# ScalarE's copies of C moved to the front of their slots, and TensorE's B of the next unit moved in front of the last tile of C

## Time and profile before

| | |
|---|---|
| median of 3 runs | 381.95 us (381.24 to 383.88) |
| the profiled execution | 382.38 us, of which the span from first to last instruction is 380.6 us |
| granted TensorE clock, mean | 0.89 |
| VectorE busy | 327.5 us, 86% |
| GpSimd busy | 279.9 us, 74% |
| TensorE busy | 265.0 us, 70% |
| ScalarE busy | 230.3 us, 61% |

### The profile page before, as it was taken

How to read it: one execution, slowest core, us unless ns; L and a number is a source line. 1 busy time by engine, 2 the same in 40 slices (tenths; PEclk the granted TensorE clock), 3 DMA queues, 4 the chain that set the end, 5 groups by cost and what they waited for, 6 DMA issues and landing times.

```text
span 380.6 us, 4003 instructions
## 1 busy us (share of the span) xinstructions
PE 265.0 (70%) x1130; PEld 124.4 (33%) x1130; DVE 327.5 (86%) x365; ACT 230.3 (61%) x509; POOL 279.9 (74%) x167
## 2 busy tenths in 40 slices
PE   2557659678856788688868786878688570692791
PEld 1113123213311335133613361336223340361491
DVE  4875979999999998989999988899889999458970
ACT  3453754955596459754996488657964573154434
POOL 0092655687588998899889998998899898614642
PEclk9859898789989999789999998799969895697887
DMA  3750470190028002720092008300730000000001
GB/s 63 158 119 1 89 160 2 26 199 23 2 54 192 6 0 54 168 55 2 12 205 59 2 0 189 87 2 2 156 92 2 0 0 28 0 3 28 0 2 55
DMA packets 19246, 21.86 MB, mean 57 GB/s; under 512 B 6096, under 2 KB 15128, under 8 KB 19224
## 3 DMA queue, kind: packets, MB, share of 16 engines
q1 hardware_dynamic: 18504, 21.05, 24.4%
q10 hardware_dynamic: 720, 0.56, 0.8%
HBM read 2.72 MB, written 2.10 MB: 13 GB/s over the span
## 4 chain that ended last, share of the span: by engine, by line
PE 30%; DVE 22%; ACT 19%; issue 12%; POOL 10%; SPq 4%; DMA 3%; DVEq 0%; POOLq 0%; ACTq 0%
DVE states L1018 8%; PE ps_prep L1314 7%; DVE db L1002 5%; PE ps_b L1321 5%; ACT c_rep L559 3%; ACT ps_decay L483 3%; PE ps_y L1280 3%; SPq L440 3%; PE ps_prep L1301 3%; POOL product L756 3%; PE ps_f L1346 2%; POOL hq L812 2%; ACT r_feat L567 2%; DMA dt_rep<-dtx 2%; DVE hidden L1068 2%
## 5 line engine op out<-in xcount | busy, mean ns | idle before, releaser
L756 POOL TENSOR_TENSOR product<-states,c_rep 128x1024 f32<-128x1024 f32 x63 | 149.3, 2375 | 30.7 <-DVE states L1018 28.9
L483 ACT ACTIVATE ps_decay<-dt_rep,aneg 128x512 f32<-128x512 f32 x128 | 87.4, 692 | 43.0 <-DVE states L1018 39.9
L1002 DVE SCALAR_TENSOR_TENSOR db<-ps_b,bbc_rep,dt_rep 128x2048 f32<-128x2048 f32 x31 | 72.5, 2339 | 11.2 <-PE ps_b L1321 8.4
L1018 DVE TENSOR_TENSOR_SCAN states<-ps_decay,states,db 128x512 f32<-128x512 f32 x64 | 79.0, 1260 | 2.4 <-POOL product L756 2.4
L1018 DVE TENSOR_TENSOR_SCAN states<-ps_decay,db 128x512 f32<-128x512 f32 x64 | 75.4, 1203 | 0.4 <-ACT ps_decay L483 0.2
L1314 PE MATMUL ps_prep<-u_feat,wbc_rep 128*128 128x512 f32 x56 | 37.1, 749 | 21.0 <-ACT c_rep L559 20.9
L1321 PE MATMUL ps_b<-u_feat,wbc_rep 128*128 128x512 f32 x64 | 40.4, 719 | 15.4 <-DVE db L1002 15.4
L1280 PE MATMUL ps_y<-product,gather 128*32 128x512 f32 x256 | 36.3, 642 | 0.8 <-POOL product L756 0.8
L1346 PE MATMUL ps_f<-gate_t,xq_t 128*128 128x352 f32 x56 | 24.5, 519 | 10.2 <-DVE hidden L1068 6.1
L597 ACT ACTIVATE gate_tanh<-ps_f 128x352 f32<-128x352 f32 x28 | 13.0, 465 | 27.9 <-PE ps_f L1346 27.9
L559 ACT ACTIVATE c_rep<-ps_prep,bbc_rep 128x512 f32<-128x512 f32 x28 | 19.4, 694 | 16.7 <-PE ps_prep L1314 16.1
(11 more groups left out here) (202 smaller groups left out, 513.1 us busy)
## 6 DMA issues: line engine op xcount, KB each, us to landing
dt_rep<-dtx SPq DMA_DIRECT2D x124, 128.0 KB, 2.4
x_tok<-in_L_attn_x SPq DMA_DIRECT2D x8, 256.0 KB, 3.1
out<-y_out SPq DMA_DIRECT2D x8, 256.0 KB, 2.3
dt_rep<-dtx ACTq DMA_DIRECT2D x4, 128.0 KB, 3.7
hidden<-in_L_ffn_w_down SPq DMA_DIRECT2D x1, 176.0 KB, 3.6
x_feat<-in_L_attn_x SPq DMA_DIRECT2D x8, 0.5 KB, 2.7
hidden<-in_L_ffn_w_gate SPq DMA_DIRECT2D x1, 128.0 KB, 2.8
hidden<-in_L_ffn_w_up SPq DMA_DIRECT2D x1, 128.0 KB, 2.5
```

Source lines behind the costliest of these rows:

```text
L483: nc.scalar.activation(ps_decay[BANK_OF[k]][:], dt_rep[p][:, c, 0, :], ACT.Exp, scale=aneg[:, c, m:m + 1]).then_inc(decay_done, 1)
L756: nc.gpsimd.tensor_tensor(product[:, j % PRODUCTS], states[p][:, first:first + 2, :], over(c_rep[p][:, j // SET_PAIRS, :], 2), ALU.mult).t ...
L1002: nc.vector.scalar_tensor_tensor(out=db[m % DB][:], in0=over(ps_b[:], QUADS), scalar=bbc_rep[:, 0, m:m + 1], in1=dt_rep[p][:, :, 1, :], op ...
L1018: nc.vector.tensor_tensor_scan(out=states[p][:, k % ring, :], data0=ps_decay[BANK_OF[k]][:], data1=db[k // QUADS % DB][:, k % QUADS, :], i ...
```

## The change

ScalarE: in slots 8 to 11 (`AT["act C"]`) `prep`, the copy of a tile of C, is emitted right after the decay (and, in the first step, the first unit's C and the weights), ahead of `gate`, `square_x`, `square_h` and `down`. In all other slots `prep` stays last. TensorE: B of set 0 of the next unit moves from slot 11 to slot 10. As `spread_b` is the first call of a slot, it then stands between tile 2 of C (slot 9) and tile 3 of C (slot 10).

```diff
-    "pe x": 0, "pe conv": (1, 2), "pe z": 4, "pe B": (11, 15, 3, 7), "pe C": (7, 8, 9, 10),
+    "pe x": 0, "pe conv": (1, 2), "pe z": 4, "pe B": (10, 15, 3, 7), "pe C": (7, 8, 9, 10),
...
+                    if a is not None and k in AT["act C"]:
+                        prep(a, 1 - p, k)
                     if f is not None:
                         gate(f, k)
...
                     if h is not None:
                         down(h, 1 - p, k, ps_f2)
-                    if a is not None:
+                    if a is not None and k not in AT["act C"]:
                         prep(a, 1 - p, k)
```

## The result

The changed kernel took 391.65 us (median of 4 runs, 391.21 to 392.58) beside 382.25 us for the kernel before (4 runs, 381.24 to 383.88): a ratio of 1.0226 [1.0191, 1.0262] (in brackets, here and below, the 95% interval). The forecast was 386.3 us with 389.0 as its upper end. Six further runs of the same changed kernel had a median of 389.46 us (386.80 to 393.40), ratio 1.0131 [1.0073, 1.0189]. It is slower in both, and it spreads over 6.6 us.

The account below looks back on a forecast made before the run. No engine was full; VectorE was taken as the bound, with GpSimd's hq close behind, both releasing TensorE's slot 2 transposes. Terms 0.4 + 1.65 + 0.35 + 1.2 + 0.7 = +4.3 us gave 386.3 us, range 380.8 to 389.0.

Parts of the forecast that it names:

- The sign: Whole kernel: the change makes it slower, by +4.3 us; slower was given 0.5.
- the place: ScalarE's slot 8: the square and variance start 1.57 us late, felt at TensorE's transposes of slot 2.
- the chain: C0's wait delays square and variance, then VectorE's qh_magic and GpSimd's norm, slot 10 and hq, then TensorE's slot 2 transposes.
- No step in front of u1 changes: Step of u0: nothing changes, as its B was waiting behind a DMA anyway; 0 us.
- u1, C1 ahead of `square_x`, +0.4: Step of u1: C1's copy makes square_x late for VectorE, which has no wait to absorb it until u2; +0.4 us.
- u2, all of the stall at `qh_magic` goes into `hq`, +1.65: Step of u2: square_h waits for C0, VectorE stalls at qh_magic, GpSimd's hq takes it all; +1.65 us.
- `hq` 1.14 to 1.21 us late from u3 on: GpSimd from u3: late variance delays norm and slot 10, hence hq; steps +0.35 (u3), +1.2 (u4), +0.7 us (u5).
- "+0 to +1.65 us is luck", the clock: TensorE's C2, B and C3 at half clock: u3, u5, u6 cost +0.9 us each, +1.65 in all; 388 us, chance 0.2.
- B's new wait for `db` costs 0: TensorE's slot 10: B now waits for VectorE's db of set 3, but C2 ends later than that; 0 us.
- u6 to the end, 0: After u6: -1.3 for B, +0.65 for the square, u7's late products take back the rest; -0.65 to +0.9, taken as 0.
- Rival A: GpSimd's gaps swallow norm's delay before slot 2, so VectorE keeps B's gain: 379 to 380 us; chance 0.12.
- Rival B: C0's matmuls come 0.9 us earlier against ScalarE, so the copy costs only 0.57 us: 382 us; chance 0.18, shared with another rival.

Follow-up runs that it names:

- e8: The whole changed kernel run again, nothing altered: 389.46 us, ratio 1.0131 to the kernel before.
- e2: Kernel before with only B of the next unit moved to TensorE's slot 10, ScalarE's old order: 382.32 us, ratio 0.9953.
- e7: Changed kernel with the matmul of C1 issued twice on TensorE: 394.65 us, ratio 1.0289 to the kernel before.
- e3: Changed kernel, but C0's copy last again in slot 8; C1 to C3 first, B in slot 10: 383.82 us, ratio 0.9995 to the kernel before.
- e1: Changed kernel with B back in slot 11, so only ScalarE's new order: 390.21 us, ratio 1.0142 to the kernel before.
- e4: Kernel before with only C0's copy moved first in ScalarE's slot 8: 393.48 us, ratio 1.0257.
- e10: Changed kernel with slot 8 ordered variance, C0's copy, square_h: 398.16 us, ratio 1.0372 to the kernel before.
- e5: Changed kernel with slot 8 ordered square_h, C0's copy, variance: 382.73 us, ratio 0.9978 to the kernel before.
- e6: Changed kernel with C0's matmuls issued one slot earlier on TensorE, ScalarE's new order kept: 382.02 us, ratio 0.9972 to the kernel before.
- e9: Kernel before with B in slot 10, variance ahead of square_h, and VectorE's qx_magic ahead of the scan in slot 10: 377.02 us, ratio 0.9802.
- e11: e2 run again (only B moved to slot 10 of the kernel before): 381.32 us, ratio 0.9950.
- e12: e9 with qx_magic back behind the scan of slot 10: 383.98 us, ratio 0.9993 to the kernel before.

## Why the prediction was wrong

The sign, the place and the chain were right; the size was too small, and the time fell outside the range. The step that failed is TensorE's clock: put at nothing in front of u1, and from u3 on looked for in one stretch only, at a chance of 0.2 (1 and 5 below). In the profile of the change it made 3.6 us in front of u1 and 1.66 us at the gate. The other term that was clearly too small is u2 (3).

1. *No step in front of u1 changes.* It held for the order of the work, not for the time. The 3.6 us there in the first profile were the clock (0.62 instead of 0.89), as e8 shows. I had read this part off one execution and kept no room for it in the range, although it is nearly as large as the forecast itself. Whether the other three runs of the result had it too is not shown, as only one was profiled.
2. *u1, C1 ahead of `square_x`, +0.4:* +0.20 measured.
3. *u2, all of the stall at `qh_magic` goes into `hq`, +1.65:* +2.35. The stall was as said (1.53 us), but I priced `qh_magic` at its old length. In the profile after, VectorE and GpSimd in u2:

```profile
120.41 1.29 DVE L964 TENSOR_SCALAR qh_magic<-qh_magic 128x1408 bf16<-128x1408 bf16 x1 [1.53 <-ACT qh_magic L610]
```

```profile
118.97 2.36 POOL L758 TENSOR_TENSOR product<-states,c_rep 128x1024 f32<-128x1024 f32 x1
```

   Delayed, it fell into the product and took 1.29 us, 0.74 more than the 0.55 of the earlier trace rows, ending 0.37 us after the product. With its start 1.60 us later against `u_feat` than before (13.47 and 11.87 us) that makes 2.34; the step grew by 2.35.
4. *`hq` 1.14 to 1.21 us late from u3 on:* the mechanism was right, the term a little large. Slot 10 moved from 17.57 (e2) to 18.40 us behind `u_feat`, +0.83; `var_eps` took 0.20 us and not the 0.49 that I had carried along. The 0.49 was a block as well, in the other direction: `var_eps` ended at 154.85 us, 0.06 us after VectorE's `qh_magic` (154.29 + 0.50), and a delayed `var_eps` misses it. These 0.29 us are nearly the whole difference. A step that `hq` holds is 39.34 us in e2 and 40.16 in the changed kernel: +0.82. This term I had over-charged.
5. *"+0 to +1.65 us is luck", the clock:* this is the step that failed, together with 1. I looked for a fall of the clock over C2, B and C3 only, priced it at 0.9 us, in u3, u5 and u6, and gave it 0.2. What happened is another stretch: the clock is low over gate, up projection and B, and the tanh of the gate is late for `hidden`. In the first profile that made u3 and u4 0.77 and 0.89 us longer; in e7, at 0.56, it made +1.64 us. (The case that I had priced, C3's copy and y in front of `xq_t` at a low clock, exists too: e3 has it in u4 and u5, at 40.48 and 40.36 for the 39.34 of e2, 1.1 us and not 0.9.) That the 1.66 us of the first profile equal my +1.65 is luck: other steps, another stretch. In e8 and e1 it struck the step of u2 (41.88 and 41.90 us). It is no symmetric luck either. The gate's first matmuls took 1.54 us and not 0.86 in 7 of the 30 steps u2 to u6 of the six profiles in which VectorE waits for the square (the changed kernel, e1, e4, e7, e8, e10), and in none of the 40 of the eight others (the kernel before, e2, e3, e5, e6, e9, e11, e12). In the stretch from 22 to 28 us the granted clock was 1.00 in all these steps of e2, e3, e5, e6, e11 and e12; but it was also 0.95 and 0.91 in u3 and u6 of the kernel before and 0.72 in u2 of e9. The lowest of the six were 0.54 to 0.84. Taking each step at the shortest seen in the two profiles of the changed kernel, 34.91 + 31.18 + 36.56 + 40.32 + 40.34 + 40.45 + 40.16 + 121.4 = 385.3, and 1.8 around it, gives 387.1 us, and its fastest run took 386.80. My 386.3 was a forecast of the best case.
6. *B's new wait for `db` costs 0:* held in time, not in fact. In u2 VectorE ran late and B waited for it, 1.27 us (1.3 to 2.4 us in u3 to u6 of e10), but `hq` closed that step. In the later steps it was 0.
7. *u6 to the end, 0:* +0.9, the end that I had given as the bound.
8. *Rival A* (GpSimd has room) is refuted by e4, where C0 alone is moved: 393.48 us for 384.38. The 0.83 us of slot 10 reach the end of the step in full (0.82). *Rival B* comes out in e5 and e6, where the wait is taken away: 0.9978 and 0.9972.

The terms with what they measured: 0.2 + 2.35 for u1 and u2; 3 × 0.82 = 2.46 less 1.02 for B from u3 to u5; 0.9 at the end: 4.9 us at full clock. The gate's clock adds 0.77 and 0.89 in u3 and u4 of the profiled execution (40.93 and 41.05 for 40.16), which makes its 6.5; the medians lay 5.5 us (389.46 for 383.96) and 9.4 us (391.65 for 382.25) above the kernel before. The share of the clock is worked out from single steps; what makes it fall at the gate stays open. Each slow gate stood behind a wait for `xq` of 0.6 to 2.9 us; but behind waits of the same 2.06 us the gate ran at 1.00 in e5 and e6, and in u3 and u5 of e7, so the idleness alone doesn't decide it.

## What to carry to other kernels

On an in-order queue an instruction that has to wait hands its wait on to the readers of everything behind it: ask who reads the next two results, not only who reads this one. The cure is to make its input earlier (e6) or to put work that is read at once ahead of it (e5); a new order can cost more than the wait did (e10). A sum made at full clock is the lower end: in these profiles the clock only added to it, by up to 3.6 us in front of u1 and 1.6 us in a later step, and the range belongs above it. And an edit that gains nothing alone (e12) may gain as one of a pair (e9), since alone it only uncovers the next wait.

## What the runs showed of the hardware

**VectorE and GpSimd block each other.** The bf16 `qh_magic` takes 0.50 to 0.53 us alone. Started 1.44 us into a GpSimd product of 2.36 us it took 1.29 us, started 0.36 us into one it took 2.37 us; both ended 0.37 to 0.38 us after the product. By its length it didn't run slower, it began after the product. The other way round, GpSimd's `var_eps` takes 0.20 us alone; started 0.07 to 0.16 us into `qh_magic` (u3 to u6 of the kernel before) it took 0.41 to 0.49 us and ended 0.06 to 0.07 us after it. The Trainium skill (SBUF — State Buffer, "🔬 SBUF: two separate sides") says that the two engines share a pair of ports as an exclusive lock, held for a whole instruction, when VectorE's instruction runs in a mode that uses both ports or reads two inputs from SBUF, and that the later one blocks fully. The rows agree with the block; they don't show VectorE's mode. The cost to bear in mind is the other instruction's remaining length, here up to 1.9 us for an instruction of half a microsecond.

**The clock falls in pieces of a step.** The same instructions of e7 took 1.02 and 1.91 us for B at a clock of 1.00 and 0.56 (the 2.4 GHz level throughout, and mostly the 1.2 GHz one), in two steps that were alike up to that point; the step closed 1.64 us later. Between two profiled executions of one kernel the first 35 us differed by 3.5 us.
